# Output tiles of a four-layer low-rank kernel: h2's table in 96 rows, part of it joined to h1's product, the rest of two tiles as two 64-row products

## The reference

```
x = x + einsum('bct,bcd->bdt', x, w0[idx])                         # layer 0: mixes a sequence's 64 rows
x = x + x @ W1 + (x @ A1[idx]) @ B1[idx]                           # layer 1: rank 16
x = x + x @ W2.T + (x @ A2[idx2]) @ B2.T * 0.5                     # layer 2: rank 32
x = x + x @ W3.T + 2 * sum_e gate_e * (x @ A3[e].T) @ B3[e].T      # layer 3: 8 experts of rank 16,
                                                                   # gates: softmax over the top 2 logits
```

## Time and profile before

| | us |
|---|---|
| median of three runs | 521.66 |
| the profiled execution | 521.29 |
| its span, first to last instruction | 519.5 |
| TensorE busy in it (2720 matmuls) | 515.0 |
| VectorE, ScalarE, GpSimd busy | 333.2, 201.9, 169.5 |

### The profile page before, as it was taken

One profiled execution on the slowest core, in us unless ns is written; L12 is line 12 of the kernel. 1 busy time (PEld: TensorE's weight loads), 2 busy tenths in 40 slices (PEclk: granted clock), 3 DMA queues, 4 the chain that ended last, 5 costly groups with the idle time before them and its releaser, 6 DMA issues.

```text
span 519.5 us, 8870 instructions
## 1 busy us (share of the span) xinstructions
PE 515.0 (99%) x2720; PEld 450.2 (87%) x2720; DVE 333.2 (64%) x655; ACT 201.9 (39%) x351; POOL 169.5 (33%) x250
## 2 busy tenths in 40 slices
PE   8999999999999999999999999999999999999997
PEld 8999999988988888888887888888888888888886
DVE  4798886799533333399876864756647557476464
ACT  5745643345223222267344233323333333233322
POOL 2550000002102020219546544444254434552400
PEclk9999999999999999999999999999999999999999
DMA  8911210214430202040703303213233032222312
GB/s 266 374 62 41 59 40 1 82 40 126 160 110 0 82 0 82 0 167 3 242 1 118 122 21 119 100 47 108 82 116 121 34 118 86 68 88 81 119 34 81
DMA packets 29631, 46.80 MB, mean 90 GB/s; under 512 B 12052, under 2 KB 17940, under 8 KB 29476
## 3 DMA queue, kind: packets, MB, share of 16 engines
q1 hardware_dynamic: 29412, 45.85, 26.8%
q0 software_dynamic: 192, 0.59, 0.3%
HBM read 33.39 MB, written 13.04 MB: 89 GB/s over the span
## 4 chain that ended last, share of the span: by engine, by line
PE 99%; DMA 0%; ACT 0%; issue 0%; POOL 0%; SPq 0%; POOLq 0%
PE bank L1892 27%; PE bank L1826 15%; PE bank L1758 11%; PE bank L1881 8%; PE bank L1800 6%; PE bank L1729 5%; PE bank L1812 5%; PE bank L1972 4%; PE bank L1940 4%; PE bank L1948 4%; PE bank L1713 3%; PE bank L1943 1%; PE bank L1942 1%; PE bank L1902 1%; DMA w2raw<-in_w_dram 0%; PE bank L1929 0%
## 5 line engine op out<-in xcount | busy, mean ns | idle before, releaser
L1892 PE MATMUL bank<-t_hi,em_hi 128*128 128x512 f32 x168 | 57.2, 403 | 0.0
L686 POOL TENSOR_TENSOR tmp<-raw 128x512 f32<-128x512 f32 x4 | 7.2, 1793 | 97.3 <-DVE raw L1368 97.3
L1182 DVE TENSOR_TENSOR w1t_lo<-raw,w1t_hi 128x1024 fp32r<-128x1024 f32 x18 | 23.7, 1316 | 23.6 <-ACT w1t_hi L911 17.1
L1892 PEld LDWEIGHTS bank<-t_hi,em_hi 128*128 128x128 f32 x168 | 31.1, 189 | 7.1 <-DVE em_hi L1182 0.4
L1826 PE MATMUL bank<-te,em_hi 128*128 128x512 f32 x144 | 34.9, 395 | 0.0
L672 POOL CAST em_hi<-tba 128x256 fp32r x32 | 13.4, 447 | 61.2 <-PE bank L1881 57.5
L1826 PEld LDWEIGHTS bank<-te,em_hi 128*128 128x128 f32 x144 | 27.0, 188 | 6.5
L1182 DVE TENSOR_TENSOR em_hi<-tmp,em_hi 128x512 fp32r<-128x512 f32 x22 | 15.1, 688 | 21.7 <-ACT em_hi L1018 12.6
L676 POOL TENSOR_TENSOR em_lo<-tba,em_hi 128x256 fp32r<-128x256 f32 x32 | 27.1, 869 | 2.4 <-POOL em_hi L672 1.2
L1758 PE MATMUL bank<-em_hi,w2s_hi 128*128 128x384 f32 x80 | 27.0, 337 | 0.0
L1758 PE MATMUL bank<-em_lo,w2s_hi 128*128 128x384 f32 x80 | 27.0, 337 | 0.0
(11 more groups left out here) (309 smaller groups left out, 1613.9 us busy)
## 6 DMA issues: line engine op xcount, KB each, us to landing
raw<-in_x_dram SPq DMA_DIRECT2D x16, 512.0 KB, 3.9
b1s<-b1scr SPq DMA_DIRECT2D x32, 217.5 KB, 2.7
raw<-in_b1w_dram SPq DMA_DIRECT2D x10, 512.0 KB, 3.2
out_dram<-ef SPq DMA_DIRECT2D x16, 256.0 KB, 2.1
out_dram<-ost SPq DMA_DIRECT2D x15, 256.0 KB, 2.4
graw<-in_w3a3wr_dram SPq DMA_DIRECT2D x4, 768.0 KB, 11.1
b1scr<-b1stage SPq DMA_DIRECT2D x12, 256.0 KB
w2raw<-in_w_dram SPq DMA_DIRECT2D x6, 384.0 KB, 6.8
```

The lines of the kernel that those rows point to most:

```text
L1182: V.tensor_tensor(dst, src, f32(hi), ALU.subtract).then_inc(signal, 1)
L1892: ins = nc.tensor.matmul(to[:, :], left[a][:, k0 + k, :], m_right(right, z, k), start=(name in OPENS and n == 0), stop=(n == 3 * KH - 1), ...
```

## The change

b2scr's third part (the low part of the first) gets the second part added, by one accumulating transfer in DRAM that POOL's queue issues behind the three stores. So h2's table has three parts of 32 rows for a tile: high, low, high. h2c's four parts become low, high, low, high of h2.

- The high part of h2 times the high part of the table is joined to h1's product: h1T and b1s grow from 96 to 128 rows, the 32 new rows (H2) of b1s hold the table, and the 32 new rows of h1T are copied by a second ACT instruction in `h2_t`.
- The other 64 rows (h2's low part times high, its high part times low) stand in b2s twice, in rows 0 to 63 and 64 to 127. `two_tiles` takes the lower half for the even tile, as the last product of its bank, and right behind it the upper half for the odd tile, as the first of its bank (`tile_low`). The very last tile, done in halves, has its own 64-row products, and the last even tile has one without a partner.
- `h2_into`, the narrow step, still uses all 128 rows of h2T; the columns of b2s beyond D are cleared by POOL first, and one of their parts stays zero.
- SP loads b2s and the new rows of b1s in seven transfers in place of one.
- The waits for the odd bank (s_yd, s_xnl) stand ahead of the couple; the wait for GHT (s_ghl) stands behind h1's product; in the first and the last pair the second block's `gated_across` moves from behind tile 0 to ahead of the couple.

```diff
+    b1s = [small(f"b1s{s}", [P, B1C], F32R) for s in range(2)]
+    h1T = [small(f"h1T{s}", [P, P], F32R) for s in range(2)]
+    H1, H2 = slice(0, 2 * SEG1), slice(2 * SEG1, P)
+    QROWS = [slice(R2 * m, R2 * (m + 1)) for m in range(4)]
...
-            sp.wait_ge(s_b2st, 16 * 3)
-            sp.dma_start(f32(b2s[:, :]), b2scr).then_inc(s_b2s, 16)
+            sp.wait_ge(s_b2st, 16 * 4)
+            sp.wait_ge(s_b2z, 1)
+            high, low = b2scr[QROWS[0], :], b2scr[QROWS[2], :]
+            sp.dma_start(f32(b2s[QROWS[0], :]), high).then_inc(s_b2s, 16)
+            sp.dma_start(f32(b2s[QROWS[1], :]), low).then_inc(s_b2s, 16)
+            sp.dma_start(f32(b2s[QROWS[2], 0:D]), high[:, 0:D]).then_inc(s_b2s, 16)
+            sp.dma_start(f32(b2s[QROWS[3], 0:D]), low[:, 0:D]).then_inc(s_b2s, 16)
+            sp.dma_start(f32(b2s[QROWS[3], D:]), high[:, D:]).then_inc(s_b2s, 16)
+            for s in range(2):
+                sp.dma_start(f32(b1s[s][H2, 0:D]), high[:, 0:D]).then_inc(s_b2s, 16)
...
+            pool.wait_ge(s_b2st, 16 * 3)
+            pool.dma_start(b2scr[QROWS[2], :], b2scr[QROWS[1], :], accum_op=ALU.add, max_dma_last_dim=4640).then_inc(s_b2st, 16)
...
+            pool.wait_ge(s_b1z, 2)
+            nc.gpsimd.memset(f32(b2s[:, D:]), 0.0).then_inc(s_b2z, 1)
...
                 nc.scalar.activation(h2T[s][:, :], bank[RT + s][0:SEG2, Z2], ACT.Copy).then_inc(s_hts, 1)
+                nc.scalar.activation(h1T[s][H2, :], bank[RT + s][H2, Z2], ACT.Copy).then_inc(s_htu, 1)
...
-                    steps.then(V.tensor_scalar(h2c[ts, 0:3, :], nar[ts, at_:at_ + R2].unsqueeze(1).to_broadcast([T, 3, R2]),
+                    steps.then(V.tensor_scalar(h2c[ts, 1::2, :], nar[ts, at_:at_ + R2].unsqueeze(1).to_broadcast([T, 2, R2]),
...
-                    V.scalar_tensor_tensor(h2c[ts, 3, :], nar[ts, at_:at_ + R2], SCALE2, f32(h2c[ts, 0, :]),
-                                           ALU.mult, ALU.subtract).then_inc(s_h2c, 1)
+                    V.scalar_tensor_tensor(h2c[ts, 0::2, :], nar[ts, at_:at_ + R2].unsqueeze(1).to_broadcast([T, 2, R2]), SCALE2,
+                                           f32(h2c[ts, 1::2, :]), ALU.mult, ALU.subtract).then_inc(s_h2c, 1)
...
             def h2_into(b, s):
                 pe.wait_ge(s_hts, 2 * b + 2)
+                pe.wait_ge(s_htu, b + 1)
...
+            def tile_mix(p, n, to, opens):
...
+                nc.tensor.matmul(to[:, :], h1T[s][:, :], b1s[s][:, cols], start=False, stop=False, skip_group_check=True)
+            def tile_gated(p, n, to, last_):
...
+            def tile_low(n, half, to, opens):
+                s, c = TILES[n]
+                rows, cols = slice(64 * half, 64 * (half + 1)), slice(c * BANK, (c + 1) * BANK)
+                return nc.tensor.matmul(to[:, :], h2T[s][rows, :], b2s[rows, cols], start=opens, stop=not opens, skip_group_check=True)
+            def two_tiles(p, s, first, last):
+                n = 2 * s
+                above(pe, s_ya, 2 * p + s)
+                tile_mix(p, n, bank[YB], True)
+                pe.wait_ge(s_ghl, 2 * p + s + 1)
+                if first and s == 0:
+                    pe.wait_ge(s_b3l, 1)
+                tile_gated(p, n, bank[YB], False)
+                if s == 0 and (first or last):
+                    gated_across(2 * p + 1, 1)
+                above(pe, s_yd, 2 * p + s)
+                if s == 0 and not last:
+                    pe.wait_ge(s_xnl, 2 * p + 3)
+                tile_low(n, 0, bank[YB], False).then_inc(s_y, 1)
+                if last and s == 1:
+                    return
+                tile_low(n + 1, 1, bank[YB + 1], True)
+                tile_mix(p, n + 1, bank[YB + 1], False)
+                tile_gated(p, n + 1, bank[YB + 1], True).then_inc(s_y, 1)
...
-                    nc.tensor.matmul(out_, h2T[s][:, :], b2s[:, cols], start=False, stop=False, skip_group_check=True)
+                    nc.tensor.matmul(out_, h2T[s][0:64, :], b2s[0:64, cols], start=False, stop=False, skip_group_check=True)
...
-                pe.wait_ge(s_b2s, 16)
+                pe.wait_ge(s_b2s, 16 * 7)
...
-                for n in range(1, 3 if last else 4):
-                    tile(p, n, False, last)
+                for s in range(2):
+                    two_tiles(p, s, False, last)
```

More of the change, by code:

```diff
@@ L45, in cond_resid_kernel @@
     NB = B // PER
+    assert 2 * 3 * R1 + R2 == P and 4 * R2 == P
     assert PER == 2 and K == 8 and D == 2 * BANK and E * R3 == P and NB % 2 == 0
@@ L242, in cond_resid_kernel @@
     q[0] = X0 + 6 * HALF
-    b1s = [small(f"b1s{s}", [2 * SEG1, B1C], F32R) for s in range(2)]
+    b1s = [small(f"b1s{s}", [P, B1C], F32R) for s in range(2)]
     b2s = small("b2s", [SEG2, D + C3], F32R)
-    h1T = [small(f"h1T{s}", [2 * SEG1, P], F32R) for s in range(2)]
+    h1T = [small(f"h1T{s}", [P, P], F32R) for s in range(2)]
+    H1, H2 = slice(0, 2 * SEG1), slice(2 * SEG1, P)
+    QROWS = [slice(R2 * m, R2 * (m + 1)) for m in range(4)]
     at_gh = q[0]
@@ L312, in cond_resid_kernel @@
         s_b2s = sem("s_b2s")
+        s_b2z = sem("s_b2z")
         s_b3 = sem("s_b3")
@@ L369, in cond_resid_kernel @@
         s_hts = sem("s_hts")
+        s_htu = sem("s_htu")
         s_ghh = sem("s_ghh")
@@ L722, in _ @@
             for s in range(2):
-                nc.gpsimd.memset(f32(b1s[s][:, D + C3:]), 0.0).then_inc(s_b1z, 1)
+                nc.gpsimd.memset(f32(b1s[s][H1, D + C3:]), 0.0).then_inc(s_b1z, 1)
+            pool.wait_ge(s_b1z, 2)
+            nc.gpsimd.memset(f32(b2s[:, D:]), 0.0).then_inc(s_b2z, 1)
             pool.wait_ge(s_s0l, 1)
@@ L1037, in h1_t @@
                 act.wait_ge(s_th, 2 * b + 1)
-                nc.scalar.activation(h1T[s][:, :], bank[RT + s][0:2 * SEG1, Z1], ACT.Copy).then_inc(s_hts, 1)
+                nc.scalar.activation(h1T[s][H1, :], bank[RT + s][H1, Z1], ACT.Copy).then_inc(s_hts, 1)
             def h2_t(b, s):
@@ L1913, in h1_into @@
                 pe.wait_ge(s_b1s[s], 64 * p + 64)
-                nc.tensor.matmul(bank[RT + s][:, 0:C3 + PER * R2], h1T[s][:, :], b1s[s][:, D:], start=False, stop=True,
+                nc.tensor.matmul(bank[RT + s][:, 0:C3 + PER * R2], h1T[s][H1, :], b1s[s][H1, D:], start=False, stop=True,
                                  skip_group_check=True).then_inc(s_small, 1)
@@ L1929, in gated_across @@
                 nc.tensor.transpose(bank[RT + s][:, Z1], gh[:, :, :].rearrange("p e r -> p (e r)"), ident[:, :]).then_inc(s_tg, 1)
-            def tile(p, n, first, last):
+            def tile_mix(p, n, to, opens):
                 s, c = TILES[n]
[L1934 to L1937, removed]
                 pe.wait_ge(s_xml, 4 * p + n + 1)
@@ L1939, in tile @@
                 for a, z in TERMS:
-                    ins = nc.tensor.matmul(to[:, :], BD[s][a][:, :], XM[n % 2][z], start=(a, z) == TERMS[0], stop=False, skip_group_check=True)
+                    ins = nc.tensor.matmul(to[:, :], BD[s][a][:, :], XM[n % 2][z], start=(opens and (a, z) == TERMS[0]), stop=False,
+                                           skip_group_check=True)
                 ins.then_inc(s_mix, 1)
+                cols = slice(c * BANK, (c + 1) * BANK)
                 nc.tensor.matmul(to[:, :], h1T[s][:, :], b1s[s][:, cols], start=False, stop=False, skip_group_check=True)
-                nc.tensor.matmul(to[:, :], h2T[s][:, :], b2s[:, cols], start=False, stop=False, skip_group_check=True)
+            def tile_gated(p, n, to, last_):
+                s, c = TILES[n]
+                cols = slice(c * BANK, (c + 1) * BANK)
+                for a, z in TERMS:
+                    ins = nc.tensor.matmul(to[:, :], GHT[s][a][:, :], B3[z][:, cols], start=False, stop=(last_ and (a, z) == TERMS[-1]),
+                                           skip_group_check=True)
+                return ins
@@ L1944, in tile @@
+            def tile_low(n, half, to, opens):
+                s, c = TILES[n]
+                rows, cols = slice(64 * half, 64 * (half + 1)), slice(c * BANK, (c + 1) * BANK)
[4 more added lines that the diff above has]
+                tile_mix(p, n, bank[YB], True)
                 pe.wait_ge(s_ghl, 2 * p + s + 1)
-                if first and n == 0:
+                if first and s == 0:
@@ L1946, in tile @@
                     pe.wait_ge(s_b3l, 1)
-                for a, z in TERMS:
-                    ins = nc.tensor.matmul(to[:, :], GHT[s][a][:, :], B3[z][:, cols], start=False, stop=(a, z) == TERMS[-1], skip_group_check=True)
-                ins.then_inc(s_y, 1)
+                tile_gated(p, n, bank[YB], False)
[4 more added lines that the diff above has]
+                    pe.wait_ge(s_xnl, 2 * p + 3)
@@ L2044, in first_pair_products @@
                 narrow(2, first_block, YB + 1)
[L2045 to L2048, removed]
+                for s in range(2):
+                    two_tiles(0, s, True, False)
             def first_block(z, k):
@@ L2128, in pair_products @@
                     gated_across(b1, 1)
```

(7 more changed lines are left out.)

## The result

The changed kernel took **531.21 us** (median of 5 runs, 529.15 to 533.12), beside 521.79 for the kernel before in the same runs: a ratio of 1.0181, 95% interval 1.0165 to 1.0197. It is slower by about 9.4 us; 521.6 was predicted, and 519.0 to 526.0 as the range. The profiled execution took 531.97 us with a span of 530.2, 10.7 more than before's 519.5.

What follows compares the result with a forecast made beforehand. TensorE's unbroken matmul stream, busy 99% of the span, was taken as the bound. Couples -3.0, h2_into +1.5 and x's stall +1.5 summed to 0.0 on the median 521.66, given as 521.6 us; range 519.0 to 526.0.

Steps and rivals of the forecast that it cites:

- The couple: Tile stage: two 64-row products stream at once in place of one h2 matmul per tile; 15 couples, -3.0 us.
- e: A couple's net price against one h2 matmul per tile before; taken as -0.20 us.
- the bounds -0.233 to +0.48: A couple's price: from both products streaming at once to two tails and the weight loads laid open.
- case C: Array empties at each change between 128 and 64 rows; slower, +4.0 in all, 525.7 us; chance 0.24.
- The stall of x: First pair's second "mixed": six added SP issues make x late, TensorE stands still, +1.5 us.
- my two values: Time from x's issue to ACT's split in the first pair: 3.9 to 4.8 us.
- the covers: Slack between x's split and TensorE's second "mixed", 0.23 and 0.54 us, taken off x's lateness of 2.3.
- The stall at h2_into: Six later pairs: TensorE comes sooner, but ACT's copies behind the store chain come 0.25 late each; +1.5 us.
- The rest, at nothing: DRAM sum on POOL, b2s clearing, DVE's h2c operations, earlier waits and DVE's eviction: taken as zero.

Runs made afterwards that it cites:

- full_late: later_copy with every 64-row product of the tiles as one of 128 rows in the same place and bank (low terms counted twice): 521.74 us, ratio 1.0008.
- later_copy: late_loads with h1T's new rows copied later on ACT, from h2T in SBUF, behind exp and the xn copy: 525.36 us, ratio 1.0067.
- one_visit_early: later_copy with the last lone products gathered, a pair's two couples in one visit, and ACT's second copy back behind h2T's: 524.57 us, ratio 1.0065.
- before_seven: The kernel before, with b2s's one load cut into seven and nothing else changed: 525.61 us, ratio 1.0075.
- x_first: The changed kernel with x's loads right behind the three table loads h2_into needs, b3raw and the other four behind: 527.92 us, ratio 1.0108.
- couple_twice: x_first with each couple done twice within one visit to the 64-row form (low terms counted twice): 532.13 us, ratio 1.0178.
- full_rows: x_first with 128-row products in place of the 64-row ones (low terms counted twice): 524.28 us, ratio 1.0060.
- late_loads: The changed kernel with fewer table loads, those only the tiles read issued behind b3raw, x and b1s: 525.10 us, ratio 1.0071.

## Why the prediction was wrong

- *The couple (e = -0.20 taken, +0.155 measured) is the step that failed.* "Two products of disjoint rows and banks share nothing that the program names" is true, and they do stream together; the boundary to the products on either side is what they share. The value was taken from the gain inside the visit, and the 0.03 for its edges was no row's. The steps say 0.39 for the edges and -0.233 inside; the bounds -0.233 to +0.48 held it. The term became +2.3 in place of -3.0, and the lone products at the end, costed only in case C, +1.0. full_late shows that the rows alone make this.
- *Case C, at 0.24, was the mechanism.* Its own term was +1.5 and +1.0; its edges were reckoned as two tails of 0.165, 0.33, and are 0.39.
- *The stall of x was placed rightly and sized wrongly*: at the second "mixed", behind x's split, exp, the gates and xn, 1.5 taken, 4.2 measured. The issue was late as forecast (3.08, of which 0.3 was there already; 2.76 taken). The load took 1.0 longer than the longer of my two values; the gates took 1.4 longer, which I had left at their old duration; the covers were 0.25 and 0.60, near the 0.23 and 0.54 taken.
- *The lower clock behind the stall, 1.4, was not in the sum.* No row of before had TensorE standing still there, and I gave a stall no price beyond its length.
- *The stall at h2_into (+1.5) did not come.* It needed TensorE to be 0.40 early at each pair's h2_into, and it came late instead. TensorE shows no wait there at all; a few weight loads stood idle for up to 0.3.
- *The rest, at nothing:* no wait in the traces names the sum in DRAM or the clearing, and DVE's h2c operations took 0.95 us for the first block in both kernels. ACT's second copy is less clear: about 1.2 of short waits at narrow and elsewhere in the changed kernel are left unexplained by couples. With the loads in order most of it is gone, copy in place, so I cannot call the copy its cause; what set these waits in the changed kernel stays open. The copy's place is not free everywhere: later_copy gained nothing from moving it, one_visit_early lost 0.8 by moving it back.

## What to carry to other kernels

Where products of fewer rows are packed side by side, count the visits to that form and not the products: each visit costs a fixed edge (0.39 us here, 1.7 slots), so gather the packed products behind one entry, or leave them at full rows. Here a couple saved one slot, so one couple a visit lost 0.155 and two gained 0.08. An issue added to a queue is paid by what is queued behind it, at the reader's end: order loads by their readers' order on the engine that takes them, and put those that nobody reads yet last. A stall of the main engine is worth more than its length if the clock falls in it.

## What the runs showed of the hardware

- Two 64-row products of 512 columns in different halves of the rows start together: the pair's row is 0.49 us, a lone one's 0.50, the next mix starts 0.43 behind either, and a second pair in the same visit adds 0.24. The Trainium skill's "TensorE: Matmul & The Clock Gate", Part 3, lets different row groups run at once; the traces agree inside a visit, and the edges above are outside of what it says.
- Weights for the other form were not loaded beside the stream: before all 16 entries in the changed kernel the weight load stood idle for about 0.35, and behind 15 exits for about 0.24. The 96-row product of the kernel before shows no such edge: the products start at 445.84, 446.07 (96 rows) and 446.30.
- After standing for 4.2 us (the change), 4.0 (before_seven, x_first) and 2.8 (couple_twice) TensorE worked at 1.2 GHz for some microseconds (granted clock down to 0.50, in couple_twice 0.53 over 266 to 268); after 0.4 us (full_rows) the clock stayed at 1.00.
- DVE's two small gm operations took 1.61 us together beside POOL's sums, 0.48 in late_loads, where POOL's sums began after them. In before_seven, again beside POOL's sums, they took 0.80 and the next step 1.18, in place of 0.17 in the kernel before. That POOL is the cause was not tested by itself.
